# Expert blocks of a decoder layer: where the expert number is loaded into a register, when the next layer's weights are read, and which engine moves the gate half of a block's weights

## The reference, cut to what matters

```python
E, K, I = 32, 4, 128
logits = x @ gate_w.T + gate_b
topk_logits, topk_idx = jax.lax.top_k(logits, K)
topk_weight = jax.nn.softmax(topk_logits, axis=-1)
# the 4,096 (token, expert) pairs, sorted by expert
gate = ragged_dot(xt, w_gate, group_sizes) + b_gate[gid]
up   = ragged_dot(xt, w_up,   group_sizes) + b_up[gid]
gate = minimum(gate, 7.0)
up   = clip(up, -7.0, 7.0)
activated = (up + 1.0) * gate * sigmoid(1.702 * gate)
outs = ragged_dot(activated, w_down, group_sizes) + b_down[gid]
y = sum over the 4 experts of a token of outs * topk_weight
```

## Time and profile before

| | |
|---|---|
| median of 3 executions | 895.39 us (892.92 to 897.91) |
| span of the profiled execution, first to last instruction | 901.4 us |
| the profiled execution's own time | no other than its span is given |
| expert stage in it | about 369 to 497 us |
| blocks 5 to 62 in it (line 1236) | 390.4 to 494.0 us |
| granted TensorE clock, mean | 0.899 of full speed |

### The profile page before, as it was taken

One profiled execution on the slowest core, in us unless ns is written; L12 is line 12 of the kernel. 1 busy time (PEld: TensorE's weight loads), 2 busy tenths in 40 slices (PEclk: granted clock), 3 DMA queues, 4 the chain that ended last, 5 costly groups with the idle time before them and its releaser, 6 DMA issues. The chain is left out here.

```text
span 901.4 us, 14567 instructions
## 1 busy us (share of the span) xinstructions
PE 741.1 (82%) x4318; PEld 531.8 (59%) x4321; DVE 705.7 (78%) x1518; ACT 559.4 (62%) x1389; POOL 517.9 (57%) x541
## 2 busy tenths in 40 slices
PE   5899999999999984499999148959999999943465
PEld 3588888888888762377777023335455555532333
DVE  6677788888888875577777437498999999679886
ACT  2545565555556551366666855788998788128385
POOL 2067777777787761355552575626889789423211
PEclk8899999999999997599999569969999999985676
DMA  8635000000001400455545330021222222010000
GB/s 322 222 133 242 2 1 1 8 7 1 8 1 30 178 7 12 158 187 145 150 143 120 87 105 11 4 116 64 101 94 94 93 94 94 6 42 0 1 17 30
DMA packets 29740, 70.53 MB, mean 78 GB/s; under 512 B 5408, under 2 KB 19424, under 8 KB 27360
## 3 DMA queue, kind: packets, MB, share of 16 engines
q1 hardware_dynamic: 25104, 57.15, 17.4%
q0 software_dynamic: 4560, 12.46, 5.6%
HBM read 59.17 MB, written 10.42 MB: 77 GB/s over the span
## 5 line engine op out<-in xcount | busy, mean ns | idle before, releaser
L1867 POOL TENSOR_TENSOR arena<-arena 128x1024 f32<-128x1024 f32 x63 | 148.5, 2383 | 44.7 <-DVE arena L1789 44.7
L1789 DVE TENSOR_TENSOR_SCAN arena<-arena,ps 128x1024 f32<-128x1024 f32 x64 | 143.7, 2277 | 11.8 <-PE ps L1511 7.7
L1532 PE MATMUL ps<-arena 128*128 128x512 f32 x256 | 120.1, 592 | 0.0
L646 PE MATMUL ps<-arena 128*128 128x128 f32 (+1 forms) x768 | 102.2, 284 | 0.9 <-PEq L374 0.9
L1087 POOL DMA_INDIRECT arena<-tokens,arena x63 | 61.6, 978 | 69.2 <-PE ps L1115 51.3
L646 PEld LDWEIGHTS ps<-arena 128*128 128x128 f32 (+1 forms) x768 | 92.7, 195 | 14.2 <-issue 12.6
L851 ACT ACTIVATE arena<-arena 128x128 f32<-128x128 f32 x256 | 99.1, 392 | 0.5 <-DVE arena L775 0.5
L859 ACT ACTIVATE arena<-ps 128x512 f32<-128x512 f32 x64 | 38.3, 598 | 87.5 <-PE ps L665 87.5
L1662 ACT ACTIVATE arena<-arena 128x1016 f32<-128x1016 f32 x64 | 72.7, 1142 | 18.7 <-DVE arena L1789 18.7
L1677 ACT ACTIVATE arena<-arena 128x256 f32<-128x256 f32 x192 | 81.7, 502 | 0.1
L906 POOL TENSOR_TENSOR arena<-arena 128x512 f32<-128x512 f32 x64 | 66.7, 1043 | 20.9 <-DVE arena L781 20.9
(11 more groups left out here) (329 smaller groups left out, 1633.2 us busy)
## 6 DMA issues: line engine op xcount, KB each, us to landing
arena<-c_rows SPq DMA_DIRECT2D x32, 512.0 KB, 3.7
arena<-in_E_gu SPq DMA_DIRECT2D x8, 1024.0 KB, 13.5
expert_out<-arena SPq DMA_DIRECT2D x63, 128.0 KB
arena<-in_E_dn SPq DMA_DIRECT2D x1, 4096.0 KB, 13.2
arena<-in_ctxT SPq DMA_DIRECT2D x2, 1024.0 KB, 6.0
arena<-in_A_o SPq DMA_DIRECT2D x1, 2048.0 KB, 15.8
arena<-in_X_o SPq DMA_DIRECT2D x1, 2048.0 KB, 23.3
arena<-in_F_w SPq DMA_DIRECT2D x2, 1024.0 KB, 9.2
```

The lines of the kernel that those rows point to most:

```text
L646: t = eng.matmul(ps[:, i % 2, j * P:(j + 1) * P], L["wq"][0:L["kc"], c, GH * g + j, :], src[0:L["kc"], c, b * P:(b + 1) * P], start=c == 0 ...
L1532: t = eng.matmul(ps[:, 2 * k + r, :], ident, half(hC[s % 4], r), start=False, stop=n == ST - 1)
L1789: eng.tensor_tensor_scan(hst[s % 4], dA[s % 4], psD[s % 2].rearrange("p k m -> p (k m)"), 0.0, ALU.mult, ALU.add).then_inc(h_ready, 1)
L1867: eng.tensor_tensor(hC[s % 4], hst[s % 4], Csb[i % 4], ALU.mult).then_inc(hC_ready, 1)
```

## The change

- The gate half of a block's weights is no longer copied by VectorE. SyncE issues a transfer from `wgu` into one of four buffers `wg_cur`, once `gate_up(s - 4)` is done. The first four are issued at the stage's start; that of block `s + 4` stands in SyncE's step `s`, behind the store of block `s - 1`, and behind it a register load for block `s + 5`. TensorE waits for that transfer's own semaphore. The up half stays with ScalarE (`wu_cur`, two buffers).
- The register loads stand behind the last use of the register that they fill, and each engine has two registers by turns. On TensorE the load of block `s` stands between `gate_up(s + 1)` and `down(s - 1)`; the move is gone. On ScalarE it stands behind the weight copy, on VectorE between `limits(s + 1)` and `gated(s)`.
- The later weights are read in eight pieces, behind the stores of blocks 4, 8, ..., 32: seven of 512 KB, and one (block 28) of two small transfers, 49 and 194 KB.

```diff
             @block.sync
             def _(eng):
+                e_g = [eng.alloc_register(f"e_g{k}") for k in range(2)]
+                def gate_owner(s):
+                    eng.reg_load(e_g[s % 2], owner_i[0:1, s:s + 1])
+                def gate_weights(s):
+                    if s >= 4:
+                        eng.wait_ge(gu_done, s - 3)
+                    e = eng.snap(e_g[s % 2], min_val=0, max_val=E - 1)
+                    eng.dma_start(wg_cur[:, s % 4],
+                                  wgu[:, :, bass.ds(e, 1), 0:I].rearrange("p c a m -> p c (a m)")
+                                  ).then_inc(wg_in[s % 4], 16)
+                loaded(eng, "wgu")
+                gate_owner(0)
+                for s in range(4):
+                    gate_weights(s)
+                    gate_owner(s + 1)
                 eng.wait_ge(spread_step, 2)
-                load(eng, "w1", w1, a["F_w1"])
-                load(eng, "w2", w2, a["F_w2"])
-                load(eng, "vecs", vecs, a["M_vec"])
-                load(eng, "w_in", w_in, a["M_in"])
-                load(eng, "w_bc", w_bc, a["M_bc"])
-                load(eng, "w_out", w_out, a["M_out"])
                 for s in range(RUNS):
                     u = s % 4
+                    if s + 4 < RUNS:
+                        gate_weights(s + 4)
+                        if s + 5 < RUNS:
+                            gate_owner(s + 5)
                     eng.wait_ge(y_ready, s + 1)
                     eng.dma_start(ys[s * P:(s + 1) * P, :], yout[:, u]).then_inc(y_out[u], 16)
+                    if s in (4, 8):
+                        c = (s - 4) // 4
+                        load(eng, "w1", w1[:, c], a["F_w1"][:, c])
...
+                    if s == 28:
+                        load(eng, "vecs", vecs, a["M_vec"])
+                        load(eng, "w_bc", w_bc, a["M_bc"])
+                    if s == 32:
+                        load(eng, "w_out", w_out, a["M_out"])
...
                 def gate_up(s):
-                    eng.wait_ge(wg_ready, s + 1)
+                    eng.wait_ge(wg_in[s % 4], 16 * (s // 4) + 16)
...
                     if s + 1 < RUNS:
                         gate_up(s + 1)
+                    if s < RUNS:
+                        down_owner(s)
                     if s >= 1:
                         down(s - 1)
-                    if s < RUNS:
-                        eng.reg_mov(e_down, e_next)
-                    if s + 1 < RUNS:
-                        eng.reg_load(e_next, owner_i[0:1, s + 1:s + 2])
...
                     if s + 2 < RUNS:
                         up_weights(s + 2)
+                        if s + 3 < RUNS:
+                            up_owner(s + 3)
                         tokens(s + 2)
...
                 for s in range(RUNS):
-                    if s + 2 < RUNS:
-                        weights(s + 2)
                     if s + 1 < RUNS:
                         limits(s + 1)
+                    if s + 2 < RUNS:
+                        load_owner(s + 2)
                     gated(s)
```

More of the change, by code:

```diff
@@ L1069, in decoder @@
         xT_done, xT_ready, gu_done = sem("xT_done"), sem("xT_ready"), sem("gu_done")
-        wg_ready, wu_ready = sem("block_gate_weights"), sem("block_up_weights")
+        wg_in, wu_ready = [sem(f"block_gate_weights{q}") for q in range(4)], sem("block_up_weights")
         gate_ready, up_ready, sig_ready = sem("gate_ready"), sem("up_ready"), sem("sig_ready")
@@ L1092, in _ @@
             def _(eng):
[L1093 to L1099 removed]
+                e_g = [eng.alloc_register(f"e_g{k}") for k in range(2)]
[13 more added lines that the diff above has]
+                    gate_owner(s + 1)
+                eng.wait_ge(spread_step, 2)
                 for s in range(RUNS):
                     u = s % 4
+                    if s + 4 < RUNS:
+                        gate_weights(s + 4)
+                        if s + 5 < RUNS:
+                            gate_owner(s + 5)
                     eng.wait_ge(y_ready, s + 1)
                     eng.dma_start(ys[s * P:(s + 1) * P, :], yout[:, u]).then_inc(y_out[u], 16)
+                    if s in (4, 8):
+                        c = (s - 4) // 4
+                        load(eng, "w1", w1[:, c], a["F_w1"][:, c])
+                    if s in (12, 16):
+                        some = slice((s - 12), (s - 12) + IC // 2)
+                        load(eng, "w2", w2[:, some], a["F_w2"][:, some])
+                    if s in (20, 24):
+                        c = (s - 20) // 4
+                        load(eng, "w_in", w_in[:, c], a["M_in"][:, c])
+                    if s == 28:
[3 more added lines that the diff above has]
+                        load(eng, "w_out", w_out, a["M_out"])
                 for u in range(4):
@@ L1126, in gate_up, with down_owner @@
                         for c in range(DC):
-                            t = eng.matmul(ps[:, 2 + d, k * I:(k + 1) * I], wcur[:, d, c, k * I:(k + 1) * I],
+                            w = wu_cur[:, d, c, :] if k else wg_cur[:, s % 4, c, :]
+                            t = eng.matmul(ps[:, 2 + d, k * I:(k + 1) * I], w,
                                            xinT[:, d, c, :], start=c == 0, stop=c == DC - 1)
                     t.then_inc(gu_done, 1)
-                e_next, e_down = eng.alloc_register("e_next"), eng.alloc_register("e_down")
+                e_down = [eng.alloc_register(f"e_down{k}") for k in range(2)]
+                def down_owner(s):
+                    eng.reg_load(e_down[s % 2], owner_i[0:1, s:s + 1])
                 def down(s):
                     d = s % 2
-                    e = eng.snap(e_down, min_val=0, max_val=E - 1)
+                    e = eng.snap(e_down[d], min_val=0, max_val=E - 1)
                     eng.wait_ge(act_ready, s + 1)
@@ L1142, in _ @@
                 loaded(eng, "wgu", "wdn")
-                eng.reg_load(e_next, owner_i[0:1, 0:1])
                 turn(0)
@@ L1186, in rows, with up_owner @@
                     eng.activation(yout[:, u], ps[:, 6 + s % 2, 0:D], ACT.Copy).then_inc(y_ready, 1)
-                e_a = eng.alloc_register("e_a")
+                e_a = [eng.alloc_register(f"e_a{k}") for k in range(2)]
+                def up_owner(s):
+                    eng.reg_load(e_a[s % 2], owner_i[0:1, s:s + 1])
                 def up_weights(s):
-                    eng.reg_load(e_a, owner_i[0:1, s:s + 1])
                     if s >= 2:
                         eng.wait_ge(gu_done, s - 1)
-                    e = eng.snap(e_a, min_val=0, max_val=E - 1)
-                    eng.activation(wcur[:, s % 2, :, I:2 * I],
+                    e = eng.snap(e_a[s % 2], min_val=0, max_val=E - 1)
+                    eng.activation(wu_cur[:, s % 2],
                                    wgu[:, :, bass.ds(e, 1), I:2 * I].rearrange("p c a m -> p c (a m)"),
@@ L1199, in _ @@
                 loaded(eng, "wgu")
+                up_owner(0)
                 up_weights(0)
+                up_owner(1)
                 tokens(0)
                 up_weights(1)
+                up_owner(2)
                 tokens(1)
@@ L1221, in owner_of, with load_owner @@
                     return eng.snap(e_w[s % 3], min_val=0, max_val=E - 1)
-                def weights(s):
+                def load_owner(s):
                     eng.reg_load(e_w[s % 3], owner_i[0:1, s:s + 1])
[L1225 to L1229, removed]
                 def limits(s):
@@ L1252, in _ @@
                 eng.tensor_scalar(bias_gu[:, :, 1], bias_gu[:, :, 1], 1.0, None, ALU.add).then_inc(bias_step, 1)
-                weights(0)
-                weights(1)
+                load_owner(0)
+                load_owner(1)
                 eng.tensor_tensor(prod, pick.rearrange("p b k e -> p (b k) e"), gw.rearrange("p b k -> p (b k)").unsqueeze(2).to_broadcast([P, NB * TOPK, E]),
```

3 lines of the change are left out of this document (2 added, 1 removed).

## The result

The changed kernel takes 932.12 us (median of 4 executions, 928.51 to 936.28), the kernel before 894.69 us in the same comparison (4 executions, 892.92 to 897.91): a ratio of 1.0387, 95% interval [1.034, 1.0433]. It is 37 us slower; 891.6 us was forecast, with 903 as the upper end.

The account below looks back on a forecast made before the run. Bound: a two-block loop of TensorE and VectorE holding TensorE's register load, 1.817 us a block. From 895.4 us, start -4.0, steady blocks -7.8 and pieces +8.0 sum to -3.8: 891.6 us, range 884 to 903.

Parts of the forecast that it names:

- the landing L: Gate transfer's time from issue to landing, taken as 2.3 us; bounds 1.7 (a store's row) and 3.7 (a 512 KB read).
- The gate transfer: Three-block loop of passes, store, issue and landing: (2.49 + L) / 3, so 1.60 us a block, bounds 1.40 and 2.06.
- the company: Other transfers sharing the DMA engines with the gate transfer; 0.6 us added to its landing for them.
- the other loop: TensorE and VectorE waiting on each other over two blocks; taken as 1.68 us a block once TensorE's register load moves.
- The pieces: Later weights on SyncE's queue delay the gate transfer behind: 1.1 us for each of seven, small one 0.3, 8.0 lost.
- the last rival: The clock falls after each piece's stall, about 1.7 us a block, seven times 12 us: 903.6 us; chance 0.07.
- The start: First blocks: gathers freed of the later weights, so the 2.77 us wait and slow clock go; 4.0 us gained.
- The register step: TensorE's load leaves the 0.72 us step from down passes to transposes (then 0.44 to 0.49); 7.8 us gained over 57 blocks.
- VectorE's copy: Removing VectorE's copy of the gate half gains nothing by itself, as VectorE idled 10.6 us in front of it.
- gate weights late in every block: Rival: landing of 2.9 to 3.3 us, 1.80 to 1.93 us a block, decides from 2.97; 900 to 907 us; chance 0.20.
- The hidden pieces: Rival: on-chip reads proceed while device-memory reads are under way, each piece costs 0.2 us; 885 us; chance 0.20.
- the third: Rival: register loads were not the cause, or come back; period stays near 1.80 us, 895.7 us, no change; chance 0.13.

Follow-up runs that it names:

- the first experiment: The kernel before, with only TensorE's register load moved to between the gate/up and the down passes: 890.61 us, ratio 0.9943.
- the eighth experiment: The changed kernel with VectorE copying the gate half as before, and the gate transfer going into buffers no engine reads: 896.17 us, ratio 0.9980.
- The seventh: The changed kernel with the pieces issued by ScalarE, on another queue than the gate transfers: 923.63 us, ratio 1.0296.
- the last experiment: The changed kernel, four gate buffers, with the transfer of block s + 6 in SyncE's step s, ahead of the store: 896.28 us, ratio 0.9967.

## Why the prediction was wrong

**The step that failed** is the landing L in "*The gate transfer.*": "Near the lower one, with 0.6 added for the company, I take L = 2.3 us: 1.60 us, under the 1.68 of the other loop." The price of 0.6 for the company was a choice, with no row behind it. Line 1103 of the changed kernel, over the stage and then from 482 to 527 us:

```profile
L1103 SPq DMA_DIRECT2D arena<-arena x63: 637/657/1120, 370.9 to 526.3; - x63
DMA to landing us min/median/max: 2.2/4.2/6.9
...
DMA to landing us min/median/max: 2.2/3.3/4.3
```

The value taken for every block, 2.3, is about the shortest of all. The two landing lines count one buffer in four, the second six transfers; by the semaphore updates the 21 transfers of that stretch have a median of 3.7 us (2.2 to 4.9). With the mean of blocks 42 to 60, 3.77, the loop of the prediction closes: from the start of the gate/up passes to the issue 0.98 + 1.11 + 0.54 = 2.63 (2.39 was counted), the landing 3.77, and 0.10 to the passes that wait for it make 6.50 for three blocks, the measured 2.17 a block. Of the 0.57 over the forecast's 1.60 the landing makes 0.49. The issue, put at 0.32 to 0.43, is 0.66 and lies inside the landing.

Of a quiet transfer the Trainium skill ("DMA: Bandwidth & Descriptors", section "Anatomy of one DMA — SWDGE (gpsimd) path") was the better guide: by its fixed 2.0 us and the bytes, 2.3 us were estimated for it alone, and the shortest landing here, 2.2, agrees, though ours is not issued by that path. What company added to it, 1.5 us in the mean of blocks 42 to 60, was taken as 0.6. The store of 1.7 us, the nearest row, was no likeness of it.

**The range** failed in a second step. The upper bound of 3.7 us was named, with 2.06 us a block for it, 57 x (2.06 - 1.817) = 13.9 us; with the pieces at 9.5 and the start at -4.0 it stands for 895.4 + 19.4 = 915. The range stopped at 903. Even 915 would not have held the time, since the pieces were too cheap as well.

**The pieces** were put at 1.1 us each; they cost 2.3. Their sum assumed 4.94 us of cover from a loop at 1.68, and a loop that is bound by the transfer itself has no cover to give. Alone they cost nothing (0.9989). The 2.3 hold the lower clock behind the longer stalls, which the last rival priced at 1.7 us a piece; how much of the 18.2 us it makes was not separated.

**The start** was put at -4.0 us. The pieces alone gave 1 us, within the uncertainty. The 2.77 us wait and the slow clock of the earlier trace rows seem to belong to that one execution: with the six loads still in front, the first experiment's profile has block 5 at 384.8 where before it was 390.4. A single profile's stall was priced as the kernel's. That the pieces leave the gathers free at the start, and what that is worth, is not shown.

**The register step** was right in kind and near in size: the step of 0.72 fell to 0.54 or less, the period to 1.703 where 1.68 was taken, 6.5 us for 7.8. In the changed kernel the load itself takes 0.31 in the median, against 0.51:

```profile
L1166 PEldq TENSOR_LOAD <-arena x63: 295/306/870, 377.6 to 530.0; - x63
```

**VectorE's copy** was put at nothing, and that is not settled. The kernel that keeps it (0.9926) and the one that replaces it by a transfer in good time (0.9935) can't be told apart, but only the second carries the transfer, whose mere presence costs some 5 us; the eighth experiment, with the copy and the transfer both, takes 0.9980. A gain of some us from the free VectorE could stand behind that, and no run has the one without the other.

**The rivals.** The first, gate weights late in every block, is what happened, by its own loop and from its own point of decision; its price of 900 to 907 stopped at L = 3.3, under the 3.77 measured, and kept the pieces at 1.3. The hidden pieces are true only of a kernel without the gate transfer. The register loads were it, which refutes the third. The clock did fall at pieces, as the fourth had it, but behind stalls of another cause, and with no piece on the way it stood at 1.00 while the period was 2.17.

**Open.** How the 1.5 us from the shortest landing to the mean of 3.77 divide among the store just ahead, the gathers and the other gate transfer was not taken apart. The seventh and the last experiment show that company delays a transfer whatever its place in the queue, but only of the pieces.

## What to carry to other kernels

Taking a copy off a compute engine that idles in front of it need not gain anything; a transfer that replaces it has a latency, and what matters is whether it is issued one latency ahead of its use: ask which event frees the buffer and which lets the transfer go, and put the issue at the first. Price such a latency as it is in company, here 3.8 us in the mean and not the quiet 2.2, and count what the issuing engine does in a block. Carry the upper bound of every unmeasured term into the range. Before a stall in a profile is counted as a gain, see that it is there in a second execution.

## What was not expected of the hardware

- An issue on SyncE of a transfer within the chip, with two runs of 512 bytes a partition, takes 0.66 us, with one run of 1 KB 0.51, a store 0.34.
- With the 16 DMA engines at a share of 0.98, and seven buffers, TensorE did not wait for the gate transfers; with them at 0.68, and the lead of three blocks, its weight loads waited 14 times in the 45 us behind the pieces, some 21 blocks.
- Behind an idle time of 8.23 us the gate/up passes took 2.04 us, near twice their 1.06 to 1.13; the granted clock was 0.50 from 393.5 to 395.6 us.
